# Four biased exponentials on ScalarE in place of a centring pass on GpSimd, in the local attention of a fused decoder

## The reference, cut to what matters

```python
sim = jnp.einsum('bhwie,bhwje->bhwij', bq, bk2) * QK_SCALE
sim = jnp.where(mask, -jnp.finfo(sim.dtype).max, sim)
attn = jax.nn.softmax(sim, -1)
out = jnp.einsum('bhwij,bhwje->bhwie', attn, bv2)
```

## Time and profile before

| | |
|---|---|
| median of 3 runs | 2233.74 us (2232.57 to 2235.25) |
| the profiled execution, its own time | 2233.84 us |
| its span in the trace | 2231.8 us |
| mean granted TensorE clock | 0.979 |
| PE busy | 2129.1 us, 95% |
| DVE busy | 1873.5 us, 84% |
| ACT busy | 1566.0 us, 70% |
| POOL busy | 1523.7 us, 68% |
| chain that ended last, by engine | PE 82%, issue 7%, POOL 4%, DVE 3%, ACT 3% |

### The profile page before, as it was taken

One profiled execution on the slowest core, in us unless ns is written; L12 is line 12 of the kernel. 1 busy time (PEld: TensorE's weight loads), 2 busy tenths in 40 slices (PEclk: granted clock), 3 DMA queues, 4 the chain that ended last, 5 costly groups with the idle time before them and its releaser, 6 DMA issues.

```text
span 2231.8 us, 52596 instructions
## 1 busy us (share of the span) xinstructions
PE 2129.1 (95%) x15920; PEld 1746.6 (78%) x15920; DVE 1873.5 (84%) x4540; ACT 1566.0 (70%) x4085; POOL 1523.7 (68%) x1418
## 2 busy tenths in 40 slices
PE   6999899999899999899999899999999999999997
PEld 3444478888788888788888788887788887788886
DVE  6566799999599998699997799996799996899995
ACT  4577667777577776577776677776677776677775
POOL 3344577777477777477775677775677774777773
PEclk9799899999999999999999999999999999999999
DMA  4000000000100000100000100000100000100001
GB/s 112 4 6 4 29 7 1 0 0 1 49 2 0 0 0 1 49 1 0 0 0 11 40 1 0 0 0 11 40 1 0 0 1 11 40 0 0 0 1 32
DMA packets 27983, 25.36 MB, mean 11 GB/s; under 512 B 10224, under 2 KB 25418, under 8 KB 26826
## 3 DMA queue, kind: packets, MB, share of 16 engines
q1 hardware_dynamic: 27850, 23.72, 3.4%
HBM read 22.66 MB, written 1.05 MB: 11 GB/s over the span
## 4 chain that ended last, share of the span: by engine, by line
PE 82%; issue 7%; POOL 4%; DVE 3%; ACT 3%; SPq 0%; DMA 0%; DVEq 0%; POOLq 0%; ACTq 0%
PE pv_ps L454 13%; PE s_ps L437 10%; PE proj_ps L418 9%; PE pt_ps L446 8%; PE tr_ps L428 8%; PE y_ps L472 7%; PE proj_ps L420 6%; PE proj_ps L419 6%; PE y_ps L464 3%; PE s_ps L519 3%; PE s_ps L637 2%; POOL w_lo L1445 2%; POOL s_sb L1467 1%; POOL f_lo L1562 1%; PE s_ps L513 1%
## 5 line engine op out<-in xcount | busy, mean ns | idle before, releaser
L1455 POOL TENSOR_TENSOR qk<-by_cos,by_sin 128x512 f32<-128x512 f32 x388 | 498.4, 1285 | 142.6 <-DVE by_sin L1045 111.9
L1462 POOL TENSOR_TENSOR qk<-qk,inv_norm 128x512 f32<-128x512 f32 x388 | 404.6, 1044 | 212.5 <-ACT inv_norm L775 205.1
L1467 POOL TENSOR_TENSOR s_sb<-s_sb,row_max 128x512 f32<-128x512 f32 x384 | 400.0, 1042 | 80.5 <-DVE row_max L1076 80.0
L454 PE MATMUL pv_ps<-v,p_T 128*128 128x65 f32 x3072 | 385.9, 269 | 0.0
L454 PEld LDWEIGHTS pv_ps<-v,p_T 128*128 128x128 f32 x3072 | 373.3, 192 | 0.0
L1045 DVE TENSOR_TENSOR by_cos<-proj_ps,tab 128x512 f32<-128x512 f32 x364 | 250.0, 687 | 81.8 <-ACT square L769 77.3
L446 PEld LDWEIGHTS pt_ps<-ident,p_sb 128*128 128x128 f32 x1792 | 215.6, 143 | 127.2 <-issue 38.7
L795 ACT ACTIVATE p_T<-pt_ps 128x512 f32<-128x512 f32 x448 | 266.5, 595 | 51.5 <-PE pt_ps L446 49.3
L446 PE MATMUL pt_ps<-ident,p_sb 128*128 128x128 f32 x1792 | 280.0, 280 | 21.1 <-ACT p_sb L791 17.4
L437 PE MATMUL s_ps<-k_T,q_T 64*128 64x128 f32 x3072 | 277.8, 300 | 18.1 <-issue 16.1
L418 PE MATMUL proj_ps<-w_hi,x_hi 128*128 128x512 f32 x546 | 273.0, 500 | 4.9 <-DVE by_sin L1045 2.7
(11 more groups left out here) (167 smaller groups left out, 4081.1 us busy)
## 6 DMA issues: line engine op xcount, KB each, us to landing
w_raw<-in_L_ffn_Wqkv SPq DMA_DIRECT2D x7, 1536.0 KB, 6.6
wo<-in_L_ffn_Wo SPq DMA_DIRECT2D x7, 512.0 KB, 3.8
w_raw<-in_L_ffn_W SPq DMA_DIRECT2D x7, 341.0 KB, 5.6
c_in<-in_ctx SPq DMA_DIRECT2D x16, 64.0 KB, 1.8
xn<-in_fside_BxS SPq DMA_DIRECT2D x1, 1024.0 KB, 6.3
out<-z SPq DMA_DIRECT2D x4, 256.0 KB, 3.0
w<-in_L_ffn_W SPq DMA_DIRECT2D x12, 64.0 KB
w<-in_L_ffn_W SPq DMA_DIRECT2D x7, 42.5 KB
```

Source lines behind the costliest of these rows:

```text
L454: mm = pe.matmul(pv_ps[:, (DH + 1) * j:(DH + 1) * (j + 1)], p_T[:, g % 2, j, :], v[par][:, GH * g + j, :], start=True, stop=True)
L1455: pool.tensor_tensor(heads(qk[:, c, :]), heads(by_cos[:, c % 2, :]), heads(by_sin[:, c % 2, :])[:, :, ::-1, :], ALU.add).then_inc(qk_added, 1)
L1462: pool.tensor_tensor(ap, ap, inv_norm[:, c, :].unsqueeze(2).to_broadcast([128, 8, DH]), ALU.mult).then_inc(qk_ready, 1)
L1467: pool.tensor_tensor(s_sb[:, g % 2], s_sb[:, g % 2], row_max[:, g % 2, :].unsqueeze(2).to_broadcast([128, GH, NT]), ALU.subtract).then_inc ...
```

## The change

The row maximum is written negated. The centring on GpSimd, its semaphore and the semaphore's initial increment go. ScalarE's one exponential of 128x512 becomes four of 128x128, one per head, each with its column of the negated maximum as bias; it waits for `max_ready` where it waited for `centered`. Only the last of the four increments `p_ready`. The scores in `s_sb` stay as `mask` wrote them.

```diff
@@ exps, ScalarE
             def exps(T, g):
-                act.wait_ge(centered, T * 4 + (g + 1))
+                act.wait_ge(max_ready, T * 4 + (g + 1))
                 act.wait_ge(pt_full, T * 4 + (g - 1))
-                act.activation(flat(p_sb[:, g % 2]), flat(s_sb[:, g % 2]), ACT.Exp).then_inc(p_ready, 1)
+                for j in range(GH):
+                    last = act.activation(p_sb[:, g % 2, j, :], s_sb[:, g % 2, j, :], ACT.Exp, bias=row_max[:, g % 2, j:j + 1])
+                last.then_inc(p_ready, 1)
@@ row_maxima, VectorE
-                dve.tensor_reduce(row_max[:, g % 2, :], s_sb[:, g % 2], AX, ALU.max).then_inc(max_ready, 1)
+                dve.tensor_reduce(row_max[:, g % 2, :], s_sb[:, g % 2], AX, ALU.max, negate=True).then_inc(max_ready, 1)
@@ GpSimd
-            pool.sem_inc(centered, 4 * NB)
-            def center(T, g):
-                pool.wait_ge(max_ready, T * 4 + (g + 1))
-                pool.tensor_tensor(s_sb[:, g % 2], s_sb[:, g % 2],
-                                   row_max[:, g % 2, :].unsqueeze(2).to_broadcast([128, GH, NT]), ALU.subtract).then_inc(centered, 1)
@@ slot, GpSimd
                         elif front_on:
                             scale_rotated(T + 1, g - 1)
-                        center(T, g)
                         if not front_on and 1 <= g < 3:
```

More of the change, by code:

```diff
@@ L196, in build @@
         max_ready = sem("max_ready")
-        centered = sem("centered")
         p_ready = sem("p_ready")
```

## The result

The changed kernel takes 2409.5 us (median of 6 runs, 2401.5 to 2414.5), the kernel before, beside it, 2231.4 us (2224.2 to 2235.3). The ratio is 1.0796, 95% interval 1.0775 to 1.0818: 8% slower. 2412 us had been forecast, between 2345 and 2480. One execution of a control kernel further down, 5125 us at a granted clock of 0.408, was disturbed and is left out of that kernel's figures.

A forecast was written before the change was run, and what follows sets the result against it. TensorE's queue was taken to set the slots' 17.5 us. Per layer 28.0 + 1.6 + 1.3 = 30.9 us lost, less 1.1 gained, nets 29.8; six layers add 179 to 2233.8 us: 2412 us, range 2345 to 2480.

The forecast's parts named there:

- the rival of the clock: TensorE's idle time lowers its granted clock to a mean of 0.85 in the slots: 2680 us; chance 4%.
- the rival of an earlier start: The four exponentials start during TensorE's wait, not held by `qk_out`, leaving the time at 2233 us; chance 2%.
- The price of the four exponentials: On ScalarE, four biased 128x128 exponentials at a pitch of 0.29 us take 1.26 us where 0.625 stood.
- the bias column is not paid again: Exponentials directly following each other on ScalarE have a pitch of 0.20 us, 1.0 us in all: 2315 us; chance 7%.
- no overlap: The four exponentials on ScalarE do not overlap, pitch 0.39 us: 108 us more, 2520 us; chance 5%.
- The step: From first exponential to TensorE's `values` 1.82 us; a slot's four steps grow by 0.55, 0.53, 0.43 and 0.53 us.
- The edge: Layer's end: two groups after slot 14 lose 0.635 us each; slot 15's three groups behind the centring gain 1.1 us.
- ScalarE's wait less 0.635: Slot 15: each group gains this or TensorE's wait, whichever is less: 0.17 + 0.73 + 0.18 = 1.1 us.
- What hides the centring: In the slots the exponential waits for `qk_out`, not GpSimd, so removing the centring's 4.2 us a slot brings nothing there.
- no added time: If the exponentials end as early as before, slot 15 gains at most 1.8 us a layer, 11 us: 2223 us; 2%.
- The loop that nothing gives back: Next step's exponentials stand behind `qk_out`, which waits for TensorE's delayed transposes, so 2.04 us a slot is not recovered.
- The tightest slack: Norm of chunk 3, behind the exponentials on ScalarE: 0.13 us of slack less 0.10 still leaves it free.

The follow-up runs named there:

- a control kernel further down: Kernel before with centring and subtraction of the maximum left out, one 128x512 exponential without bias in the old place: 2215.6 us, ratio 0.9931.
- the two places of the fifth exponential: Changed kernel plus one biased 128x128 exponential per group: between `qk_out` and the four, 2525.5 us; ahead of `qk_out`, 2413.6 us.
- the run with a semaphore per head: Changed kernel, but each of the four exponentials increments `p_ready` and TensorE waits for each head's: 2346.6 us, ratio 1.0510.
- the early order: Changed kernel with each group's four exponentials ahead of `qk_out`: 2225.0 us; with the order of before in step 0 of slot 0: 2215.9 us.

## Why the prediction was right, point by point

**The bound** was right: TensorE's queue had no idle time in the slots, ScalarE's busy share said nothing, and the place of the exponential in its queue decided. The granted clock stayed at 1.00 in the middle of a layer, so the rival of the clock is out, and the exponentials still started behind `qk_out`, so the rival of an earlier start is out too.

**The price of the four exponentials**: forecast 1.26 us at a pitch of 0.29, measured 1.27 for the four at a pitch of 0.29 to 0.30. The rivals "the bias column is not paid again" and "no overlap" are both out, by the two groups' 300 and 391 ns and by the pitch of 0.30.

**The step**: 1.82 us forecast, 1.82 measured in the step shown, 1.81 in those after 699.12 and 713.79. The fourth is off in every second slot: from 704.74 to `values` at 706.63 it is 1.89, since TensorE starts 0.13 us after the last exponential's end and not 0.06. It makes that slot 19.60 us in place of the 19.54 forecast; the slots between last 19.53. The hardware loop takes its slots in pairs, and the long step is the one in which TensorE passes from one pair to the next. That the loop's turn is the cause was not tested.

**The edge**: two groups at 0.635 us more each (0.56 to 1.20, measured 0.64), and the centring's three at 1.1 us less, measured 0.17 + 0.84 + 0.43 = 1.4 us. The gain was forecast too small: in the third group the whole wait of 0.43 us went, not the 0.18 that the rule "ScalarE's wait less 0.635" gave.

**The sum**: 179 us forecast, 178.1 between the two medians. The traces bear it out layer by layer: from the same place in one layer to the next it is 324.3 us before and 354.3 after (means of five), 30.0 us where 29.8 had been forecast. Between the two profiled executions it is only 170.6 us in all (2402.4 less 2231.8), and the difference lies in the first stage, which the change does not touch: its last exponential starts at 258.2 us before and at 249.0 after. Their windows, columns as in rows 1, before and after:

```profile
60.00:80.00 20.00, 19.73 (x76) 9.68 (x76) 8.80 (x33) 10.85 (x47) 5.64 (x6) 0.54 0.02 5
60.00:80.00 20.00, 17.77 (x102) 9.62 (x101) 13.93 (x47) 12.45 (x51) 7.88 (x8) 0.91 0.03 8
```

TensorE gets through 76 matmuls there at a clock of 0.54 and through 102 at 0.91; that the clock is what made this stage 9.2 us longer is read from these rows and was not tested. So the terms were right, but that the medians agree with the sum to 1 us is luck: the executions of the changed kernel alone go from 2401.5 to 2414.5 us.

**What hides the centring** was right where it counted: 11 us forecast for "no added time", 11.0 measured. That they agree to a tenth is luck, as the interval of the ratio goes from 7 to 17 us. **The loop that nothing gives back** was right too, and the two places of the fifth exponential show it. **The tightest slack**, the norm of chunk 3 behind the exponentials, held in the changed kernel, and gave way in the run with a semaphore per head (1.42 us from `values` to the transposes, 1.06 in both other kernels).

**Wrong**: ScalarE's busy time was to rise by 354 us and rose by 237.8. I had multiplied count by mean duration, and the overlap of neighbours, which the pitch of 0.29 had in it, counts once in busy time (486.6 us for 1536 instructions of 0.391). And the half microsecond of wait per step does not stand in the matmul rows as such (0.20 to 0.39).

## What to carry to other kernels

Before moving work to an engine with idle time, find which of its waits the idle time is and on which side of it the work would stand. Behind a wait that closes a loop with the bounding engine added time counts in full once the little slack there is used up (0.64 us more made the step 0.55 longer); ahead of it 1.3 us were free in the slots, though not at slot 0 of a layer. When a producer-consumer pair is cut into several instructions, price the fixed part of each and its operand columns, and check what is queued behind it. Then look for the order that lets the removed work pay.

## What the runs showed of the hardware

A [128,1] bias operand adds 0.09 us to an exponential of 128x128 on ScalarE (0.300 against 0.391 us), back to back too; neighbours overlap by about 0.1 us with it and without (four in 1.27 and in 0.90 us). With the early order ScalarE carries 15.8 us of work in a slot of 17.5, and TensorE is busy for all 17.50. A negated maximum costs VectorE nothing: 686 ns before and after.

The half microsecond idle in each step did not lower TensorE's clock: it stayed at 1.00 with TensorE busy for 18.4 of 19.6 us. At slot 0 of a layer it falls in both kernels (0.75 and 0.56 before; 0.76 and 0.55 from 625 to 635 us after). Of the changed kernel's executions the shortest had a mean clock of 0.989 and the longest one of 0.979, but 2410.5 and 2410.9 us came at 0.987 and 2404.3 at 0.988, so the mean clock does not explain all of the 0.5% between them.
